# Cross-attention on one core: the products of gU and the low part of ctxT cut to 64 rows, two heads side by side

## What is computed

```python
Q = (x @ Wq).reshape(B, -1, H, D)          # x: (8, 256, 256)
K = (ctx @ Wk).reshape(B, -1, H, D)        # ctx: (8, 256, 192)
V = (ctx @ Wv).reshape(B, -1, H, D)
attn = softmax(where(mask, Q @ K^T / sqrt(D), -inf))
out = (attn @ V) @ Wo + x
out = layernorm(out) * gamma + beta
```

## Time and profile before

| what | value |
|---|---|
| median of three runs | 317.23 us |
| the profiled execution's own time | 317.46 us |
| its span, first to last instruction | 315.7 us |
| TensorE matmul busy | 308.8 us, 98% |
| TensorE weight load busy | 302.7 us, 96% |
| VectorE busy | 253.1 us, 80% |
| ScalarE busy | 222.1 us, 70% |
| GpSimd busy | 181.4 us, 57% |
| mean granted TensorE clock | 0.997 of full speed |

### The profile page before, as it was taken

The page is one execution under the profiler, slowest core; times in us unless marked ns, Lnnn a source line. Parts: engine busy times, 40 slices in busy tenths (PEclk is TensorE's granted clock), DMA queues, the critical chain, the costliest instruction groups (busy, mean ns, idle before and its releaser), DMA issues.

```text
span 315.7 us, 8051 instructions
## 1 busy us (share of the span) xinstructions
PE 308.8 (98%) x2584; PEld 302.7 (96%) x2584; DVE 253.1 (80%) x721; ACT 222.1 (70%) x601; POOL 181.4 (57%) x183
## 2 busy tenths in 40 slices
PE   8999999999999999999999999999999999999993
PEld 7898889999999999999999999999999999999992
DVE  0467778777999879987998889987998889985686
ACT  2446678768867787678777797678767887777640
POOL 1123476457864587558855586458755686457212
PEclk9999999999999999999999999999999999999998
DMA  7995443464354553474445544364355535440101
GB/s 248 373 408 228 137 151 117 158 217 135 92 168 139 199 165 129 145 246 136 133 125 193 184 138 162 128 216 156 110 191 153 199 103 185 143 158 2 35 0 66
DMA packets 46912, 50.27 MB, mean 159 GB/s; under 512 B 3505, under 2 KB 37041, under 8 KB 46897
## 3 DMA queue, kind: packets, MB, share of 16 engines
q1 hardware_dynamic: 46608, 49.56, 46.7%
q10 hardware_dynamic: 288, 0.52, 0.7%
HBM read 32.24 MB, written 17.83 MB: 159 GB/s over the span
## 4 chain that ended last, share of the span: by engine, by line
PE 95%; DMA 2%; DVE 1%; SPq 1%; POOLq 0%; issue 0%; POOL 0%
PE score_bank L325 25%; PE out_bank L325 19%; PE gL_bank L325 14%; PE tL_bank L325 13%; PE tU_bank L325 9%; PE gU_bank L325 7%; DMA wq_raw<-in_wqT 2%; PE spare_bank L325 1%; PE spare_bank L359 1%; PE tL_bank L359 1%; PE tL_bank L341 1%; PE tU_bank L341 1%; PE tU_bank L365 1%; PE out_bank L365 1%; PE out_bank L341 0%; PE spare_bank L341 0%
## 5 line engine op out<-in xcount | busy, mean ns | idle before, releaser
L1021 POOL TENSOR_TENSOR probs<-probs,inv_sum 128x512 f32<-128x512 f32 x64 | 66.7, 1043 | 84.0 <-DVE inv_sum L808 83.4
L619 ACT ACTIVATE probs<-neg_scores,neg_max 128x256 f32<-128x256 f32 x128 | 64.2, 503 | 36.8 <-DVE neg_max L797 36.7
L1044 POOL TENSOR_TENSOR pT_lo<-pT_raw,pT_hi 128x512 fp32r<-128x512 f32 x60 | 76.7, 1298 | 8.6 <-ACT pT_hi L576 8.6
L797 DVE CUSTOM_DVE_ANT_0 neg_scores<-score_bank,mask_bias 128x256 f32<-128x256 f32 x128 | 49.2, 421 | 6.5 <-PE score_bank L325 4.0
L818 DVE STREAM_TRANSPOSE squares<-probs 128x512 f32<-128x512 f32 x60 | 42.4, 706 | 0.2
L576 ACT ACTIVATE tL_hi<-tL_bank 128x512 fp32r<-128x512 f32 x31 | 18.5, 598 | 28.4 <-PE tL_bank L325 28.4
L325 PE MATMUL score_bank<-ctxT_hi,gU 128*128 128x256 f32 x128 | 36.4, 284 | 0.0
L325 PE MATMUL score_bank<-ctxT_hi,gL_hi 128*128 128x256 f32 x128 | 36.0, 281 | 0.0
L325 PE MATMUL score_bank<-ctxT_lo,gU 128*128 128x256 f32 x128 | 35.9, 281 | 0.0
L325 PE MATMUL score_bank<-ctxT_hi,gL_lo 128*128 128x256 f32 x128 | 35.9, 280 | 0.0
L325 PE MATMUL score_bank<-ctxT_lo,gL_hi 128*128 128x256 f32 x128 | 35.8, 280 | 0.0
(11 more groups left out here) (167 smaller groups left out, 980.6 us busy)
## 6 DMA issues: line engine op xcount, KB each, us to landing
scratch<-squares SPq DMA_DIRECT2D x30, 512.0 KB, 2.7
pT_raw<-scratch SPq DMA_DIRECT2D x120, 128.0 KB, 2.9
xT_raw<-in_xT SPq DMA_DIRECT2D x8, 256.0 KB, 4.4
ctxT_raw<-in_ctxT SPq DMA_DIRECT2D x8, 256.0 KB, 4.6
wo_raw<-in_wo SPq DMA_DIRECT2D x4, 512.0 KB, 13.7
x_res<-in_x SPq DMA_DIRECT2D x8, 256.0 KB, 3.0
out<-y_out SPq DMA_DIRECT2D x7, 256.0 KB, 2.5
wq_raw<-in_wqT SPq DMA_DIRECT2D x3, 512.0 KB, 7.6
```

What stands on the lines that cost most here:

```text
L619: nc.scalar.activation(probs[j % 2][:, n, :], neg_scores[:, n, :], ACT.Exp, bias=neg_max[:, n:n + 1], scale=-1.0, accum_out=row_sum[:, n:n ...
L797: nc.vector.tensor_tensor_reduce(out=neg_scores[:, n, :], in0=score_bank[hh][:, q, :], in1=mask_bias[:], scale=-SCALE, scalar=3.0e38, op0= ...
L1021: nc.gpsimd.tensor_tensor(probs[j % 2][:, rows, :], probs[j % 2][:, rows, :], inv, ALU.mult) \
L1044: nc.gpsimd.tensor_tensor(pT_lo[j % 2][:, k].rearrange("p hh (q i r) -> p (hh q) i r", q=QT, i=ROWS), pT_raw[j % 2][:, k].rearrange("p i n ...
```

## The change

In `scores` the products of gU and ctxT_lo no longer take all 128 rows. Only the 64 rows that hold the high part of gU are used: partitions 0 to 63 for head 0, partitions 64 to 127 for head 1, so lo x lo is left out. These four matmuls (two query tiles, two heads) stand first in the phase, head 0 and head 1 in turn, and write to two different banks. The other sixteen matmuls follow as before, over 128 rows. Both waits that stood ahead of the first matmul still do; the wait for the low part of gL stands ahead of the same matmul as before. The flag that starts a bank anew is now set on the first of the four in each bank only.

```diff
-            def scores(t, j, b, heads=(0, 1)):
+            def scores(t, j, b):
 
                 if j == 0:
 
                     pe.wait_ge(ctxT_split, b + 1)
-                for hh in heads:
-                    if hh == 0:
-
-                        pe.wait_ge(g_hi_done, 3 * t + 3)
-                        pe.wait_ge(g_split, 3 * t + 2)
+                pe.wait_ge(g_hi_done, 3 * t + 3)
+                pe.wait_ge(g_split, 3 * t + 2)
+
+                for q in range(QT):
+                    rows = slice(q * P, (q + 1) * P)
+                    for hh, part in enumerate((slice(0, UP), slice(UP, P))):
+                        split_products(score_bank[hh][:, q, :], [(gU[part, hh, rows], ctxT_lo[part, 1, :])],
+                                       first=q == 0, last=False, shared=True)
+                for hh in range(2):
                     for q in range(QT):
                         rows = slice(q * P, (q + 1) * P)
                         hi, lo, up = gL_hi[:, hh, rows], gL_lo[:, hh, rows], gU[:, hh, rows]
                         split_products(score_bank[hh][:, q, :],
-                                       [(up, ctxT_hi[:, 1, :]), (up, ctxT_lo[:, 1, :]),
-                                        (hi, ctxT_hi[:, 0, :]), (hi, ctxT_lo[:, 0, :])], last=False)
+                                       [(up, ctxT_hi[:, 1, :]), (hi, ctxT_hi[:, 0, :]), (hi, ctxT_lo[:, 0, :])],
+                                       first=False, last=False, shared=True)
                         if hh == 0 and q == 0:
 
                             pe.wait_ge(g_split, 3 * t + 3)
-                        ins = split_products(score_bank[hh][:, q, :], [(lo, ctxT_hi[:, 0, :])], first=False)
+                        ins = split_products(score_bank[hh][:, q, :], [(lo, ctxT_hi[:, 0, :])], first=False,
+                                             shared=True)
                     ins.then_inc(scores_done, 1)
```

## The result

The changed kernel takes 329.27 us (median of four runs, 328.94 to 329.4) against 317.33 us before: ratio 1.0374, 95% interval 1.0356 to 1.0392, 11.9 us slower. I had forecast 322.1, range 315.8 to 329.8. The sign was right; the size was 2.5 times what I had worked out.

What follows compares the result with a forecast made beforehand. TensorE's matmul stream was taken to bound the kernel. Profiled 317.46 + 5.44 for 32 steps - 0.6 for steps 1 to 3 gave 322.3; that execution being 0.23 above the median, forecast 322.1 us, range 315.8 to 329.8.

Steps and rivals of the forecast that it cites:

- What bounds the kernel: Whole kernel: TensorE's matmul stream is the time, busy 98% of the span; any slot removed or gap added moves the end one to one.
- Fewer rows save nothing, pairs save two slots: Score phase: 64-row matmuls keep the 0.1175 us slot; head 0 and head 1 side by side save 0.235 us a step.
- The sign given for it: PE timeline: two 64-row matmuls start within 0.02 us of each other, the second pair 0.11 to 0.12 later.
- C: Score phase: weight loads of a pair queue, four slots stay four and passages come on top; 329.6 us, chance 0.10.
- D: Score phase: 64-row matmuls run as full ones with idle rows, one after another, no passage; 317.2 us, chance 0.08.
- The price of the passages: Into and out of the 64-row shape: emptying and two exposed loads cost 0.405 us per step against 0.235 saved, +0.17.
- B: Score phase: 64-row matmuls run side by side without emptying the array, next loads go ahead; 309.7 us, chance 0.20.
- E: Score phase: the pipeline empties twice, 0.20 us, but next weight loads go ahead; 316.1 us, chance 0.10.
- its own case: Score phase: pairs run side by side, passages empty the array and expose loads; 318.5 to 325.5 us, chance 0.52.
- Queued behind this: nothing more: Behind the changed matmuls and their waits in the score phase, no further cost.
- Later scores of head 0: Head 0 complete after 10 slots + 0.405 us; VectorE starts up to 0.4 us later, covered by slack, costed at nothing.
- The slack of 0.37 us: Step 12: VectorE finishes gL's low part at 129.51, TensorE uses it at 129.88; so not far from late.

Runs made afterwards that it cites:

- head by head: Changed kernel with its four 64-row matmuls in the order head 0, head 0, head 1, head 1 instead of in turn: 322.6 us, ratio 1.0158.
- full rows: Changed kernel with its order kept, but the four gU x ctxT_lo matmuls over all 128 rows: 324.61 us, ratio 1.0223.
- the other addresses: gL_hi, gL_lo, gU moved up 64 bytes, the 16-word gaps between heads and behind these tiles removed: kernel before 323.64 us, changed kernel 319.79 us.
- the later wait at those addresses: Kernel before with moved, close-packed weights, each head's gL_lo matmuls and TensorE's wait for gL_lo put behind that head's other eight: 314.9 us, ratio 0.9911.

## Why the prediction was right or wrong

*What bounds the kernel*: right. TensorE's stream is the time before and after, and no new wait appeared on it.

*Fewer rows save nothing, pairs save two slots*: right. The streams of the four take two slots, 0.22 us. The sign given for it was not quite right: the records of the second pair start 0.22 us behind the first, not 0.11 to 0.12, because the exposed first load lies between; the loads themselves start 0.11 apart. Rivals C and D are refuted by the same rows. C's 329.6 us lies next to the measured 329.27 by chance: its mechanism, loads one after another, is not in the trace.

*The price of the passages*: right, and nearly to the figure. Forecast 0.405 - 0.235 = 0.17 us per score phase; measured 2.52 - 2.35 = 0.17. In whole runs the 64-row shape costs 5.1 us (head by head against before, both in the fast cadence), 4.7 us (changed against full rows, both in the slow one) and 319.79 - 314.90 = 4.9 us at the other addresses, though the kernels of this last pair also differ in where gL_lo stands. Forecast 4.84. Rivals B and E are refuted: the array is empty 0.09 to 0.10 us on each side and both first loads are exposed. What fold_C shows for 64 columns holds for 64 rows, as the Trainium skill, TensorEngine Tiling (Array Packing), section Key Properties, has it: a change of mode drains. The trace agrees, with those 0.09 to 0.10 us. The speed-up of 3.07 in the Trainium skill, TensorE: Matmul & The Clock Gate, Part 3, says nothing of the passages. At two slots saved per visit they decide here: 0.40 us against 0.235. (The upper end that the prediction gives for its own case, 325.5, comes out at 325.1 from its terms; nothing rests on it.)

*"Queued behind this: nothing more"* is the step that failed. I carried the 0.113 us of the slots outside the scores over as a constant, so the sum had no term for the other 56 matmuls of a step. They cost 0.25 us a step more, 6.8 us in the 27 steps from 4 to 30, most of the 7.2 us between forecast and measurement. The run with full rows, 7.1 us slower than the kernel before, shows that the rewritten order costs this without any 64-row matmul, at the addresses the kernel has. The trace of before did show that the slot is no constant. In the earlier trace rows the scores run at 0.1175 and what follows at 0.113. And in the chain of the kernel before, behind the transposes at the end, eight tL matmuls take 0.94 us where eight took 0.91 before them, with nothing to wait for:

```profile
289.87 0.91 PE tL_bank L325 x8
...
295.12 0.94 PE tL_bank L325 x8
```

I read the 0.1175 as the price of a score matmul. But it is a mean. The first starts of a phase lie 0.12 us apart, the last ones 0.11, here in the trace of before:

```profile
131.53 0.28 PE L325 MATMUL score_bank<-ctxT_lo,gL_hi 128*128 128x256 f32 x1
131.64 0.28 PE L325 MATMUL score_bank<-ctxT_hi,gL_lo 128*128 128x256 f32 x1
131.75 0.28 PE L325 MATMUL gU_bank<-xT_hi,A_hi 128*128 128x256 f32 x1
```

In every step the stream is slow in there and is back at 113 to 114 ns by the last four. In the changed kernel, and with full rows, the last five intervals are 115 to 123 ns from step 4 on: it no longer comes back. A rival that said so, at 317.2 + 4.8 + 56 x 0.0045 x 27, some 329 us, could have been written from these rows.

*Later scores of head 0*: right at no cost. VectorE waits 6.2 us longer in total and TensorE waits for it nowhere. The slack of 0.37 us, though, was read at the matmul. What needs gL_lo is its weight load, one slot earlier, so the slack was some 0.25 us there; in step 1 of the kernel before it was gone, and the load came 0.09 us late. In the changed kernel that load had 1.0 us of slack in the same step 13.

What stays open: what in the hardware holds a cadence. The runs show that it is set by addresses and order, that a load 0.04 us late was followed by the slow one for the rest of the kernel, seven others by slow stretches, and that the later wait at those addresses left no sign of a drop in five runs, by their times and one trace. Why some stalls end in the fast cadence is not shown. A run that adds a stall to a fast kernel on purpose was not made, and which address bits matter was not mapped.

## What to carry to other kernels

Going into and out of a half-array shape cost 0.4 us per visit here (0.2 of emptiness, 0.2 of exposed loads), so by these numbers a visit has to save some four slots of 0.11 us before it gains; two are not enough, and more half-size work has to be gathered into one visit. In a kernel bound by a dense stream of matmuls, look at the distance between starts in every section, not only in the one that is changed: if the same shape shows two distances, the slot has states, and an edit's effect on the untouched matmuls needs a term of its own. Before judging such an edit, run it at one or two other paddings of its operands: here 64 bytes moved the time by 9.0 us, nearly twice what the 64-row shape itself costs.

## What the runs showed that I had not expected

- The same fp32r matmul (128 rows, 128 stationary and 256 moving columns) ran steadily at 113.3 ns or at 117.8 ns between starts, for over 200 us on end, at a mean granted clock of 0.996 to 0.999; after a shift of 64 bytes it ran at 120 ns.
- One load 0.04 us late was followed by the slow cadence to the end of the kernel, and seven loads 0.10 to 0.17 us late by the slow cadence up to the next scores.
- 64-row matmuls issued head 0, head 0, head 1, head 1 took the same 0.43 us as in turn.
- Moved weights, and the gL_lo matmuls with their wait put later, no change of work, brought 317.58 to 314.9 us.
